# One core: the key fetches for the spilled class of list 0 cover 64 nodes each instead of 8

## The reference, cut to what matters

```python
src = concatenate([edge_index[0], arange(M)]); dst = concatenate([edge_index[1], arange(M)])
e = leaky_relu(a_src[src] + a_dst[dst], 0.2)
e_max = segment_max(e, dst, M); ee = exp(e - e_max[dst])
agg = segment_sum(h[src] * (ee / denom[dst])[:, :, None], dst, M)   # and so on: LayerNorm, top 2 of 4, experts
```

## Time and profile before

| what | value |
|---|---|
| median of 3 runs | 2300.07 us (2298.7 to 2302.07) |
| span of the profiled execution | 2297.5 us (the page gives no other time for it) |
| median less span | 2.57 us |
| DVE busy | 1594.7 us, 69% |
| POOL busy | 1212.5 us, 53% |
| PE busy | 1086.1 us, 47% |
| ACT busy | 762.8 us, 33% |

### The profile page before, as it was taken

How to read it: one execution, slowest core, us unless ns; L and a number is a source line. 1 busy time by engine, 2 the same in 40 slices (tenths; PEclk the granted TensorE clock), 3 DMA queues, 4 the chain that set the end, 5 groups by cost and what they waited for, 6 DMA issues and landing times. The chain is left out here.

```text
span 2297.5 us, 16425 instructions
## 1 busy us (share of the span) xinstructions
PE 1086.1 (47%) x4821; PEld 479.8 (21%) x4821; DVE 1594.7 (69%) x3100; ACT 762.8 (33%) x1260; POOL 1212.5 (53%) x1233
## 2 busy tenths in 40 slices
PE   3897878778678887000700102433342425333330
PEld 1233343334533333000300001111111112111110
DVE  6999999995726999999209504364758384747658
ACT  4664846535345554000300002222232324222221
POOL 2000000000066777777777764777777777777771
PEclk8898878787589999555855556766676768676665
DMA  8202031021454322111221611344453535363543
GB/s 297 115 1 74 1 8 38 1 8 39 47 57 110 79 71 71 14 15 29 48 41 29 43 16 41 98 144 121 121 176 85 165 92 176 72 187 73 169 113 100
DMA packets 185735, 182.76 MB, mean 80 GB/s; under 512 B 81580, under 2 KB 164462, under 8 KB 176046
## 3 DMA queue, kind: packets, MB, share of 16 engines
q1 hardware_dynamic: 99262, 88.84, 14.4%
q0 software_dynamic: 43936, 47.85, 12.4%
q10 hardware_dynamic: 42448, 45.04, 6.4%
HBM read 105.23 MB, written 76.40 MB: 79 GB/s over the span
## 5 line engine op out<-in xcount | busy, mean ns | idle before, releaser
L519 POOL DMA_INDIRECT KC<-node_dram,KB x1026 | 1018.4, 993 | 938.8 <-DMA node_dram<-node_out 626.3
L740 PE MATMUL hidden_out<-XT,W 128*128 128x512 f32 x512 | 291.3, 675 | 540.8 <-ACT ARENA_A L956 539.9
L745 PE MATMUL hidden_out<-ARENA_A,W 128*128 128x512 f32 x512 | 264.7, 642 | 24.9 <-ACT ARENA_A L956 24.9
L956 ACT ACTIVATE ARENA_A<-hidden_out,b1c 128x512 f32<-128x512 f32 x256 | 174.2, 687 | 294.5 <-PE hidden_out L740 293.9
L740 PEld LDWEIGHTS hidden_out<-XT,W 128*128 128x128 f32 x512 | 97.3, 211 | 689.5 <-ACT ARENA_A L956 570.1
L1523 DVE TENSOR_TENSOR KB<-XG,MB 128x3072 bf16<-128x3072 f32 x20 | 67.1, 3354 | 163.5 <-DMA XG<-rest_dram,win_i 100.7
L1649 DVE TENSOR_SCALAR KB<-MB 128x16 f32<-128x16 f32 (+1 forms) x33 | 5.7, 172 | 238.3 <-DMA KC<-payload,slot_idx 126.8
L1800 DVE SCALAR_TENSOR_TENSOR XG<-XT,KB,XG 128x128 f32<-128x128 f32 x512 | 144.3, 347 | 14.9 <-DMA XT<-ye_dram 11.2
L959 ACT ACTIVATE ARENA_A<-hidden_out,b2c 128x512 f32<-128x512 f32 x128 | 87.9, 687 | 185.5 <-PE hidden_out L745 185.5
L1026 ACT ACTIVATE TA<-KB 128x400 f32<-128x400 f32 x32 | 16.2, 507 | 373.3 <-DVE KB L1656 373.2
L745 PEld LDWEIGHTS hidden_out<-ARENA_A,W 128*128 128x128 f32 x512 | 98.3, 207 | 182.4 <-ACT ARENA_A L956 103.1
(11 more groups left out here) (401 smaller groups left out, 2232.0 us busy)
## 6 DMA issues: line engine op xcount, KB each, us to landing
ye_dram<-ARENA_D ACTq DMA_DIRECT2D x32, 1024.0 KB, 4.0
XT<-ye_dram SPq DMA_DIRECT2D x32, 1024.0 KB, 13.5
KC<-node_dram,KB POOLq DMA_INDIRECT x1026
payload<-XT SPq DMA_DIRECT2D x1, 11520.0 KB
payload<-KC SPq DMA_DIRECT2D x115, 90.0 KB, 1.8
XG<-x_dram SPq DMA_DIRECT2D x32, 256.0 KB, 11.3
out_dram<-XG ACTq DMA_DIRECT2D x32, 256.0 KB, 3.4
KA<-in_L_ffn_edge_index_dram SPq DMA_DIRECT2D x1, 2048.0 KB, 9.0
```

Of the source, the lines that this page charges most:

```text
L519: pool.indirect_dma_start(row_buf[h][:, t, :], None, node_dram, bass.IndirectOffsetOnAxis(ap=KB[:, col:col + 1].bitcast(I32), axis=0)).the ...
L740: last = pe.matmul(PF[i % 2][:, :], W1[:, m // 2, (m % 2) * P:(m % 2) * P + P], XT[:, n * CHUNK:(n + 1) * CHUNK], start=True, stop=True)
L745: last = pe.matmul(PF[i % 2][:, :], W2[:, 2 * m + kk, :], HH[:, 2 * m + kk, :], start=kk == 0, stop=kk == 1)
L956: act.activation(HH[:, m, :], PF[i % 2][:, :], ACT.Gelu, bias=b1c[:, m:m + 1]).then_inc(S["hid_out"], 1)
```

## The change

For list 0 the spilled class no longer uses columns of 8 nodes. It gets two columns of 64 nodes (`WIDE_SHARE`), one batch of two fetches in the third buffer. The two batches of class 0 and everything for list 1 stay as they were. The wide batch compares 8 limits of both columns at a time (`WIDE_J`). The largest distance that sets the number of rounds is taken over the 16 narrow and the 2 wide columns together.

```diff
+WIDE_SHARE, WIDE_J = 64, 8
+WIDE_COLS = P // WIDE_SHARE
+WIDE_BATCH = WIN_BATCHES // 2
...
+        found_wide = KC[:, 904:904 + P].rearrange("p (c j) -> p c j", j=WIDE_SHARE)
+        below_wide = KB[:, HALF + 256:HALF + 256 + WIDE_J * WIDE_COLS * WINDOW // 2].bitcast(BF16).rearrange(
+            "p (j c w) -> p j c w", j=WIDE_J, w=WINDOW)
...
         def win_batches(a):
 
-            return range(a * WIN_BATCHES // 2, WIN_BATCHES)
+            return range(WIN_BATCHES // 2, WIN_BATCHES) if a else range(WIDE_BATCH + 1)
+
+        def win_cols(a, b):
+
+            return WIDE_COLS if a == 0 and b == WIDE_BATCH else WIN_COLS
...
-                        for k in range(WIN_COLS):
+                        for k in range(win_cols(a, b)):
                             col = b * WIN_COLS + k
...
-                used = slice(a * GROUPS_OF_NODES // 2, GROUPS_OF_NODES)
+                narrow = slice(a * GROUPS_OF_NODES // 2, (a + 1) * GROUPS_OF_NODES // 2)
+                beyond = slice(narrow.stop, narrow.stop + (0 if a else WIDE_COLS))
+                used = slice(narrow.start, beyond.stop)
                 first_win = shared(win_f)[:, :, 0]
-                link(cp(win_at, first_win))
-                link(tt(win_i[:, used], shared(win_f)[:, used, SHARE - 1], first_win[:, used], ALU.subtract))
+                wide_win = win_f[:, P:].rearrange("p (c j) -> p c j", j=WIDE_SHARE)
+                link(cp(win_at[:, narrow], first_win[:, narrow]))
+                link(tt(win_i[:, narrow], shared(win_f)[:, narrow, SHARE - 1], first_win[:, narrow], ALU.subtract))
+                if a == 0:
+                    link(cp(win_at[:, beyond], wide_win[:, :, 0]))
+                    link(tt(win_i[:, beyond], wide_win[:, :, WIDE_SHARE - 1], wide_win[:, :, 0], ALU.subtract))
                 red(max_deg[:, :], win_i[:, used], AX.X, ALU.max).then_inc(S["spread_ready"], 1)
...
-                        dve.wait_ge(win_in[a][b], (r + 1) * (16 * WIN_COLS))
+                        dve.wait_ge(win_in[a][b], (r + 1) * (16 * win_cols(a, b)))
+                        if a == 0 and b == WIDE_BATCH:
+                            shape = [P, WIDE_J, WIDE_COLS, WINDOW]
+                            ends = limits_p[:, P:].rearrange("p (c j) -> p j c", j=WIDE_SHARE)
+                            for j in range(0, WIDE_SHARE, WIDE_J):
+                                window_link(tt(below_wide, bc(windows[n % WIN_BUFS][:, 0:WIDE_COLS, :], 1, shape),
+                                               bc(ends[:, j:j + WIDE_J, :], 3, shape), ALU.is_lt))
+                                window_link(red(found_wide[:, :, j:j + WIDE_J].rearrange("p c j -> p j c"), below_wide,
+                                                AX.X, ALU.add))
+                            dve.sem_inc(windows_counted[a], 1)
+                            wide = counted[:, P:].rearrange("p (c j) -> p c j", j=WIDE_SHARE)
+                            window_link(tt(wide, wide, found_wide, ALU.add))
+                            continue
...
+                if a == 0:
+                    wide = lambda ap: ap.rearrange("p (c j) -> p c j", j=WIDE_SHARE)
+                    link(stt(wide(starts[:, 1, 0:P]), bc(wide_win[:, :, 0], 2, [P, WIDE_COLS, WIDE_SHARE]), float(STRIDE),
+                             wide(counted[:, P:]), ALU.mult, ALU.add))
```

More of the change, by code:

```diff
@@ L1486, in find_starts @@
                 link(ts(win_f, cum.rearrange("p g l -> p (g l)"), -1.0, 0.0, ALU.add, ALU.max))
-                used = slice(a * GROUPS_OF_NODES // 2, GROUPS_OF_NODES)
+                narrow = slice(a * GROUPS_OF_NODES // 2, (a + 1) * GROUPS_OF_NODES // 2)
+                beyond = slice(narrow.stop, narrow.stop + (0 if a else WIDE_COLS))
+                used = slice(narrow.start, beyond.stop)
                 first_win = shared(win_f)[:, :, 0]
-                link(cp(win_at, first_win))
-                link(tt(win_i[:, used], shared(win_f)[:, used, SHARE - 1], first_win[:, used], ALU.subtract))
+                wide_win = win_f[:, P:].rearrange("p (c j) -> p c j", j=WIDE_SHARE)
[4 more added lines that the diff above has]
+                    link(tt(win_i[:, beyond], wide_win[:, :, WIDE_SHARE - 1], wide_win[:, :, 0], ALU.subtract))
                 red(max_deg[:, :], win_i[:, used], AX.X, ALU.max).then_inc(S["spread_ready"], 1)
                 dve.wait_ge(S["spread_ready"], a + 1)
-                ts(win_i[:, 0:GROUPS_OF_NODES], win_at, float(window_base[a]), None, ALU.add).then_inc(win_idx_ready[a], 1)
+                ts(win_i[:, used], win_at[:, used], float(window_base[a]), None, ALU.add).then_inc(win_idx_ready[a], 1)
                 dve.wait_ge(S["spread_t"], a + 1)
@@ L1506, in find_starts @@
                 dve.sem_inc(windows_counted[a], min(WIN_BUFS, len(batches)))
-                WINDOW_OPS = len(batches) * (2 * SHARE // PAIR_J + 1) + 2
+                WINDOW_OPS = 2 * (2 * SHARE // PAIR_J + 1) + (0 if a else 2 * WIDE_SHARE // WIDE_J + 1) + 2
                 with dve.Fori(0, window_rounds(dve, a)) as r:
@@ L1526, in find_starts @@
                         window_link(tt(shared(counted[:, cols]), shared(counted[:, cols]), found, ALU.add))
-                    window_link(ts(win_at, win_at, float(SPAN), float(LIST // STRIDE), ALU.add, ALU.min))
-                    window_link(ts(win_i[:, 0:GROUPS_OF_NODES], win_at, float(window_base[a]), None, ALU.add))
+                    window_link(ts(win_at[:, used], win_at[:, used], float(SPAN), float(LIST // STRIDE), ALU.add, ALU.min))
+                    window_link(ts(win_i[:, used], win_at[:, used], float(window_base[a]), None, ALU.add))
                     assert done[0] == WINDOW_OPS
                     dve.sem_inc(win_idx_ready[a], 1)
-                for k in ((0, 1), (3,))[a]:
+                if a == 0:
+                    wide = lambda ap: ap.rearrange("p (c j) -> p c j", j=WIDE_SHARE)
+                    link(stt(wide(starts[:, 1, 0:P]), bc(wide_win[:, :, 0], 2, [P, WIDE_COLS, WIDE_SHARE]), float(STRIDE),
+                             wide(counted[:, P:]), ALU.mult, ALU.add))
+                for k in ((0,), (3,))[a]:
                     g = k % 2
```

## The result

The changed kernel takes **2640.42 us** (median of 4 runs, 2639.33 to 2641.34) against 2299.53 us for the kernel before, measured beside it. The ratio is 1.148, with a 95% interval of 1.146 to 1.150. The profiled execution has a span of 2638.5 us.

What follows compares the result with a forecast made beforehand. POOL's queue of gathers was taken as the bound, held by three more rounds of DVE: span 2297.5 + 341.9 = 2639.4 us, plus 2.57 us from span to median, 2642 us; range 2618 to 2668.

Steps and rivals of the forecast that it cites:

- The number of rounds: Window loop of list 0: a wide column reaching 9 steps makes it take 4 rounds instead of 1; chance 0.88.
- A round on DVE: DVE's comparing in one round of list 0: 110.4 us less about 0.4 for one addition of counts, 110.0 us.
- The wide shape: DVE's compares of 8 limits by 2 columns by 192: taken as no change, at most 2 us a round more.
- The restart: From a round's end to the next compare: 0.85 us to POOL's first fetch, then 12.3 us to the first compare.
- The branch backwards: Loop's return to a further round: taken as nothing, bounded above by 5.44 us.
- The period: One round of list 0 with its restart: 110.0 + 0.85 + 12.3 = 123.2 us.
- POOL's delay: POOL goes on with row gathers after list 0 at 1089.6 instead of 747.72 us, 341.9 us later.
- What is late next: At list 1 POOL stays later than DVE, whose wait of 100.66 us shrinks by 27 to some 73 us.
- The price of the row gathers beside the sort: POOL's 333 gathers beside list 1's sort take 1.116 us against 0.950 each; this price is neither saved nor paid twice.
- One round: Rival: wide columns of list 0 need one round, so POOL is free 28.5 us earlier, 2271.6 us; chance 0.05.
- Another number of rounds: Rivals for list 0: three rounds, 2518.7 us, chance 0.04; a fifth round, 2765 us, within the 0.03 for others.
- a stage that absorbs part: Rival: slack behind 1198 us takes up part of POOL's delay; within the 0.03 for others.

Runs made afterwards that it cites:

- e2: Changed kernel with the number of rounds taken from the narrow columns alone, so list 0 has one round: 2270.52 us, ratio 0.988.
- e4: Kernel before, one round, but DVE compares the last batch of list 0 13 times instead of once: 2535.50 us, ratio 1.103.
- e5: Changed kernel with columns of 32 nodes and windows of 384 keys for list 0's spilled class, one round: 2268.68 us, ratio 0.987.

## Why the prediction was right, point by point

Predicted were 2642 us, measured 2640.42, inside 2618 to 2668.

**The number of rounds** was the step on which all hung. It came from the data, and the counts of pairs agree: 40 narrow pairs (32 for list 0 in four rounds, 8 for list 1) and 32 wide ones. The reference's edges give the 130,947 ordinary and 16,509 spilled keys of list 0 and the one wide column of 9 steps; only partition 25, which should have had no spilled key, has 2, and nothing hangs on them.

```profile
L1551 DVE TENSOR_TENSOR KB<-XG,MB x40: 3353/3355/3356, 710.7 to 1598.1; 128x3072 bf16<-128x3072 f32 x40
```

```profile
L1539 DVE TENSOR_TENSOR KB<-ARENA_Y,MB x32: 3353/3355/3355, 765.8 to 1181.0; 128x3072 bf16<-128x3072 f32 x32
```

**A round on DVE.** The wide shape was priced as no change, 3.35 us an operation; the rows above show 3.355. DVE's first round took 110.11 us, from 710.75 to 820.86, against 110.41 in the earlier trace rows; priced were 110.0.

**The restart** was priced a little too high: 0.85 us and 12.3 us, 13.15 together. Measured is 0.95 us from the end of L1557 to POOL's first fetch (820.86 to 821.81) and 11.51 us from there to the compare (821.81 to 833.32), 12.46 together: the price of list 1, and not the mean of the two lists that the sum took. The earlier trace rows could have told it: 7 x 1.254 us from the first fetch to the eighth and the median of 2.8 us from there to landing are 11.6 us. The branch backwards, for which no row stood, shows no more than 0.1 us, by the 0.95 us against the 0.85 of a wait without one. By the Trainium skill's estimate of 2.2 us for a fetch (DMA: Bandwidth & Descriptors, on the anatomy of one DMA on the SWDGE path), put behind the end of the eighth, the first compare would have come 7 x 1.254 + 0.95 + 2.2 = 11.9 us behind the first fetch, nearer than my 12.3. Measured are 11.51, of which 1.8 us lie behind the end of the eighth fetch, or 2.7 behind its start. The period came out at 122.6 instead of 123.2 us.

**POOL's delay** was 341.9 us by the sum and is 1089.53 - 747.72 = 341.8. Small errors cancel in it: the first compare came 1.0 us later (710.75 against 709.77), DVE's three rounds took 0.4 us more together, and the two restarts were 0.7 us cheaper each. That the sum meets the measurement to 0.1 us is therefore luck; it is good to about 1 us.

**What is late next.** DVE was forecast to wait 73 us at list 1 and waited 73.10. The price of the row gathers beside the sort was to stay the same, and did: the 333 of them took 448.9 us, from 1089.53 to the end of the last at 1538.47, against 450.0 before. Everything behind shifted whole: the last row gather's DMA stands 341.1 us later, and the span is 341.0 us longer.

**The rivals.** One round would have been a gain of 28.2 us (e2). Another number of rounds did not come, nor a stage that absorbs part. Of the 1.6 us between forecast and median, 0.9 lie in the span (2639.4 forecast), the rest in what lies around it: 1.9 us here, where I had put 2.57.

## What to carry to other kernels

Before a fetch is made to cover more, work out from the data how far it has to reach, and look for a loop whose trip count follows the worst column: here one column of 64 nodes, 9 steps long, made all columns go round four times. Count the waits that a loop puts into an engine's queue, and not its instructions: POOL's 40 more DMAs are 50 us of its queue, its three waits 303 us, and everything behind the loop stood meanwhile. Then ask what the other engine's longer loop would cost without these waits: here some 281 us, by the estimate under e4. Size the window with the share (32 nodes and 384 keys), and the fewer fetches pay, until the other engine's slack is used up.

## What the runs showed of the hardware that I had not expected

How much POOL's gathers slow beside DVE depends on what DVE runs. POOL by line in the changed kernel, 1090 to 1190 us, beside the compares, and 1192 to 1459 us, beside the sort of list 1 (busy us, mean ns, idle before):

```profile
L529 POOL DMA_INDIRECT KC<-node_dram,KB x81 | 76.6, 946 | 24.7 <-issue 24.7
```

```profile
L529 POOL DMA_INDIRECT KC<-node_dram,KB x189 | 210.3, 1113 | 57.6 <-issue 57.6
```

The compare has one input in SBUF and one in MB, which is PSUM, and costs POOL nothing; most sort steps have two inputs in SBUF, and beside the sort a gather takes 0.17 us more in the mean. With the sort moved away from most of them, in e4, POOL's 333 row gathers took 417.0 us (748.41 to 1165.38) instead of 450.0. The Trainium skill (SBUF — State Buffer, section on who interferes with whom) tells these two cases apart: a DVE instruction with at most one input in SBUF, outside its two-port modes, does not contend with GpSimd, one with two contends with a GpSimd instruction that reads SBUF. The trace agrees on which one costs, by the 946 and 1113 ns above; that the second input is the cause no run isolates, since copies and scalings stand in the sort too.

The mean of 0.17 us comes from short steps, mostly of 0.45 to 0.8 us. Beside a long one with two inputs in SBUF a single gather took 2.75 us and ended 0.82 us after that step (start, us, instruction):

```profile
1652.95 2.29 DVE L1660 TENSOR_TENSOR ARENA_Y<-XG,KC 128x2048 f32<-128x2048 f32 x1
```

```profile
1653.31 2.75 POOL L529 DMA_INDIRECT KC<-node_dram,KB  x1 [0.30 <-issue]
```

A fetch of 384 keys for each of 128 partitions keeps POOL as long as one of 192: the median is 0.946 us for either in e5, so its price on POOL goes by the fetch and not by its bytes.
